# Linear attention over 64 images: context in 64-column tiles, attention in 64x64 tiles, one masking operation a group, and the copy of k moved ahead of the copy of v

## The reference, cut to what matters

```
q, k, v = split(rmsnorm(layernorm(h)) @ w_qkv)           # 4 heads of 32 channels, 64 tokens
k = softmax over tokens of concat(mem_k (4 columns), k)  # 68 columns
v = concat(mem_v, v)
q = softmax over the 32 channels of a head, * 32**-0.5
context = einsum('bhdn,bhen->bhde', k, v)                # 32x32 for each head and image
out = einsum('bhde,bhdn->bhen', context, q)
h = h + rmsnorm(out @ w_out + b_out) + layernorm(h)
```

## Time and profile before

| | us |
|---|---|
| median of 3 runs | 4284.08 (4277.56 to 4299.02) |
| the profiled execution | 4291.21 |
| its span, first to last instruction | 4289.4 |
| attention stage, from first `project` to last `take_out` | 3661.59 to 3784.66 |
| PE busy in the whole span | 3236.5 (75%) |
| mean granted clock of TensorE, as a share of 2.4 GHz | 0.882 |

### The profile page before, as it was taken

How to read it: one execution, slowest core, us unless ns; L and a number is a source line. 1 busy time by engine, 2 the same in 40 slices (tenths; PEclk the granted TensorE clock), 3 DMA queues, 4 the chain that set the end, 5 groups by cost and what they waited for, 6 DMA issues and landing times. The chain is left out here.

```text
span 4289.4 us, 122178 instructions
## 1 busy us (share of the span) xinstructions
PE 3236.5 (75%) x54724; PEld 2080.3 (48%) x54724; DVE 2394.2 (56%) x3232; ACT 2090.2 (49%) x1756; POOL 28.9 (1%) x48
## 2 busy tenths in 40 slices
PE   5968866667888566687876666878869996759777
PEld 4746644456555344575554444755542221743532
DVE  3456669963666589645655996456540001454556
ACT  2123345521666555216765553166659996222322
POOL 0000000000000000000000000000000001000000
PEclk8989988888999889899998898999989998669688
DMA  8979887879999877799998786999985441012053
GB/s 314 349 196 248 226 266 276 300 287 356 364 383 374 307 284 297 272 354 364 391 379 310 290 310 269 357 358 385 387 318 207 179 165 66 1 28 53 1 106 64
DMA packets 181647, 1119.64 MB, mean 261 GB/s; under 512 B 25561, under 2 KB 31905, under 8 KB 107326
## 3 DMA queue, kind: packets, MB, share of 16 engines
q1 hardware_dynamic: 140988, 843.27, 54.3%
q10 hardware_dynamic: 39234, 269.45, 18.1%
q0 software_dynamic: 1024, 1.05, 0.1%
HBM read 708.56 MB, written 405.14 MB: 260 GB/s over the span
## 5 line engine op out<-in xcount | busy, mean ns | idle before, releaser
L604 PEld LDWEIGHTS bank<-fb,arena 64*64 64x64 f32 x16384 | 670.0, 199 | 521.8 <-issue 507.7
L604 PE MATMUL bank<-fb,arena 64*64 64x128 f32 x16384 | 675.4, 294 | 244.8 <-ACT arena L661 196.2
L661 ACT ACTIVATE arena<-bank,pwb 128x1024 f32<-128x1024 f32 x512 | 559.1, 1111 | 475.7 <-PE bank L595 351.3
L705 DVE BATCH_NORM_STATS2 stats<-arena 128x6 f32<-128x512 f32 x1024 | 629.0, 676 | 191.1 <-ACT arena L661 190.8
L595 PE MATMUL bank<-arena,wst 64*64 64x512 f32 x4096 | 625.6, 635 | 12.9 <-issue 12.8
L843 ACT ACTIVATE arena<-arena,shift,scale 128x1024 f32<-128x1024 f32 x384 | 443.7, 1229 | 324.9 <-DMA arena<-y_dram 324.7
L697 DVE STREAM_TRANSPOSE arena<-bank 128x512 f32<-128x512 f32 x512 | 321.1, 684 | 454.2 <-PE bank L581 454.2
L653 ACT ACTIVATE arena<-arena,shift,scale 128x2048 f32<-128x2048 f32 x192 | 401.5, 2093 | 320.0 <-issue 206.1
L805 PE MATMUL bank<-arena,fwq 32*32 32x512 f32 x6144 | 285.2, 746 | 333.6 <-DVE arena L848 333.6
L444 PE MATMUL bank<-arena 64*64 64x128 f32 x8192 | 453.9, 393 | 103.4 <-DVE arena L471 83.6
L444 PEld LDWEIGHTS bank<-arena 64*64 64x64 f32 x8192 | 397.5, 154 | 159.5 <-issue 112.2
(11 more groups left out here) (195 smaller groups left out, 2475.9 us busy)
## 6 DMA issues: line engine op xcount, KB each, us to landing
arena<-y_dram SPq DMA_DIRECT2D x224, 2048.0 KB, 10.3
y_dram<-arena ACTq DMA_DIRECT2D x256, 1024.0 KB, 13.4
arena<-in_w_modes SPq DMA_DIRECT2D x32, 2048.0 KB, 17.5
arena<-spec_in SPq DMA_DIRECT2D x32, 2048.0 KB, 14.6
spec_out<-arena SPq DMA_DIRECT2D x128, 512.0 KB, 14.8
arena<-spec_out SPq DMA_DIRECT2D x116, 512.0 KB, 16.5
spec_in<-arena SPq DMA_DIRECT2D x24, 2048.0 KB, 13.6
spec_in<-arena SPq DMA_DIRECT2D x4, 4096.0 KB, 12.0
```

The costliest lines, as they stand in the source:

```text
L604: mm = pe.matmul(hpx(bank[4 + T % 2 * 2 + i][CHAN[v], :])[:, :, j * S:(j + 1) * S], a2[p % 2][CHAN[i], v, :, 4 * T + j], hpx(fb2[CHAN[i], :]),
L661: act.activation(hpx(yout[u])[:, :, T * BK:(T + 1) * BK], banks[:, 4 + T % 2 * 2:6 + T % 2 * 2, :], ACT.Identity, bias=pwb[:]).then_inc(y_ ...
L705: dve.bn_stats(stats[:, p * 48 + 6 * t:p * 48 + 6 * t + 6], hpx(yout[p % 2])[:, i, T * BK:(T + 1) * BK]).then_inc(y_seen, 1)
```

## The change

Four edits, all in the attention stage.

1. `context` makes for each image two products instead of one, for the heads 0, 1 and the heads 2, 3. Each has 64 columns of k as weights and 64 columns of v moving, and they lie in the two column tiles of the array. All 8 images fit in bank 0. Products of heads of different pairs are no longer computed.
2. `attend` makes for each image two products of 64x64 weights in the tiles (0, 0) and (64, 64), the first into bank 2, the second into bank 3.
3. `mask_context` is one operation of 128x512 numbers, with a mask `pairmask` of 64 columns that DVE makes once ahead of the stage. `copy_att` becomes two operations of 64 partitions each.
4. On ACT `copy_kT(n)` stands behind `copy_att(n-1)` and ahead of `values(n+1)`, instead of at the head of the next turn.

```diff
             def project(g):
                 if g > 1:
                     pe.wait_ge(qT_scaled, g - 1)
-                    pe.wait_ge(ctx_masked, 2 * g - 2)
-                    pe.wait_ge(att_copied, g - 1)
+                    pe.wait_ge(ctx_masked, g - 1)
+                    pe.wait_ge(att_copied, 2 * g - 2)
...
             def context(g):
                 for b in range(GI):
-                    mm = pe.matmul(lane_bank[u][3 * (b // 4)][:, b % 4 * HID:(b % 4 + 1) * HID], kTs[u][:, b, :], vkv[u][b // 4][0:C + MEM, b % 4, :],
-                                   start=True, stop=True)
+                    for a in range(2):
+                        mm = pe.matmul(lane_bank[u][0][ROW[a], b * C:(b + 1) * C], kTs[u][:, b, ROW[a]],
+                                       vkv[u][b // 4][0:C + MEM, b % 4, ROW[a]], start=True, stop=True, tile_position=(0, a * C))
...
             def attend(g):
                 for b in range(GI):
-                    mm = pe.matmul(lane_bank[u][2][:, b * S:(b + 1) * S], ctx_s[u][:, b, :], qT[u][:, b * S:(b + 1) * S], start=True, stop=True)
+                    for a in range(2):
+                        mm = pe.matmul(lane_bank[u][2 + a][ROW[a], b * S:(b + 1) * S], ctx_s[u][ROW[a], b, :],
+                                       qT[u][ROW[a], b * S:(b + 1) * S], start=True, stop=True, tile_position=(a * C, a * C))
...
-                act.activation(attT[u], lane_bank[u][2], ACT.Copy).then_inc(att_copied, 1)
+                for a in range(2):
+                    act.activation(attT[u][ROW[a]], lane_bank[u][2 + a][ROW[a]], ACT.Copy).then_inc(att_copied, 1)
...
             for n in range(TG + 1):
-                if n > 0:
-                    copy_kT(n - 1)
                 if n < TG:
                     exps(n)
                 if n > 0:
                     copy_att(n - 1)
+                if n < TG:
+                    copy_kT(n)
                 if n + 1 < TG:
                     values(n + 1)
...
+            dve.tensor_tensor(pairmask, headmask[:, ROW[0]], headmask[:, ROW[1]], ALU.add).then_inc(mem_max, 1)
...
-                for i in range(2):
-                    dve.tensor_tensor(ctx_s[u][:, 4 * i:4 * i + 4, :], lane_bank[u][3 * i].rearrange("p (b x) -> p b x", b=4),
-                                      row4(headmask, 4, HID), ALU.mult).then_inc(ctx_masked, 1)
+                dve.tensor_tensor(ctx_s[u], lane_bank[u][0].rearrange("p (b x) -> p b x", b=GI),
+                                  row4(pairmask, GI, C), ALU.mult).then_inc(ctx_masked, 1)
```

More of the change, by code:

```diff
@@ L1163, in build @@
         kTs = lanes(GI, HID, parts=C + MEM)
-        ctx_s = lanes(GI, HID)
+        ctx_s = lanes(GI, C)
+        pairmask = at(next_free[0], C)
+        next_free[0] += C
         qs, qT, attT = lanes(4, HID), lanes(BK), lanes(BK)
@@ L1253, in attend @@
                 pe.wait_ge(qT_scaled, g + 1)
-                pe.wait_ge(ctx_masked, 2 * g + 2)
+                pe.wait_ge(ctx_masked, g + 1)
                 for b in range(GI):
-                    mm = pe.matmul(lane_bank[u][2][:, b * S:(b + 1) * S], ctx_s[u][:, b, :], qT[u][:, b * S:(b + 1) * S], start=True, stop=True)
+                    for a in range(2):
+                        mm = pe.matmul(lane_bank[u][2 + a][ROW[a], b * S:(b + 1) * S], ctx_s[u][ROW[a], b, :],
+                                       qT[u][ROW[a], b * S:(b + 1) * S], start=True, stop=True, tile_position=(a * C, a * C))
                 mm.then_inc(att_done, 1)
@@ L1260, in project_out @@
                 u = g % 2
-                pe.wait_ge(att_copied, g + 1)
+                pe.wait_ge(att_copied, 2 * g + 2)
                 for t in range(4):
@@ L1331, in vector_attention @@
                 dve.tensor_tensor(sq[:, h], x_tok[:, h], red[:, 7, h].unsqueeze(2).to_broadcast([P, NT // 2, C]), ALU.mult).then_inc(x_ready, 1)
-            dve.wait_ge(mem_max, 1)
+            dve.wait_ge(mem_max, 2)
             k_of = lambda u: lane_bank[u][1].rearrange("p (b n) -> p b n", b=GI)
```

## The result

| | before | changed |
|---|---|---|
| median of 20 runs, us | 4294.09 (4271.38 to 4306.87) | 4273.86 |
| ratio to before, 95% interval | | 0.9948 (0.9932 to 0.9964) |
| profiled execution, us | 4291.21 | 4278.1 |
| its span, us | 4289.4 | 4276.3 |
| attention stage in it, us | 123.1 | 100.9 |

The change makes the kernel 0.52% faster, 0.36% to 0.68% with the interval. One of the 20 runs of the changed kernel took 10508.57 us and is no part of the ratio; the median of the other 19 is 4271.37 us. In a second series, of 12 runs, the ratio was 0.9957 (0.9935 to 0.9979).

What follows compares the result with a forecast made beforehand. PE was taken as the bound, with handoffs to DVE (mask) and ACT (copy of k). Turns -9.2 us, first context 1.4 us earlier, tail +0.4, `pairmask` +0.2: taken as -10, from 4284.1 to 4274 us, range 4254 to 4290.

Steps and rivals of the forecast that it cites:

- The sum of work at 1.2 GHz: Attention stage: 13.57 us a turn, 9.66 us without project; 91.1 us against 100.26 us from first to last context.
- Context, 2.1 to 2.2 us at 1.2 GHz: Context in 32 records of 64 columns: 2.1 to 2.2 us against 3.65; at 2.4 GHz 1.1 to 1.3 against 2.05.
- Attend 2.0 us: Attend in 32 records of 64x64 weights, 0.0625 us each: 2.0 us against 3.43 us at 1.2 GHz.
- tiles that wait for each other: Rival: tiles of context and attend do not run side by side, 3.8 us each; +18 us, 4302 us; chance 0.05.
- The mask's wait 0.88 us: Between context and attend: one mask operation cuts 1.48 to 0.88 us; at 2.4 GHz DVE is late, mask starts at 2.15 us.
- turn_k waits for the exponentials: After attend: turn_k can start at 5.2 us, attend ends at 5.1 us; 0.1 us of the gain is lost.
- The wait for the copy of k goes: Ahead of context: waits for ACT of 0.94 us and first 1.4 us go; nothing gained in turns at 0.50.
- A change of tile shape: Between products of different tile shapes on PE: costs at most 0.19 us; two new ones a group would be 0.4 us.
- changes paid in full: Changing the tiling mode drains the array: by that rule the two changes a group make the gain 3 us smaller.
- The clock at 0.50 throughout: Attention stage: PE stays at 0.50 of 2.4 GHz from the first context on, turns of 13.4 to 13.9 us; chance 0.5.
- the clock rises in every turn: Rival, attention stage: turns of 10.9 us, -28 us, 4256 us, chance 0.2; in half of the turns 4265 us.
- a stage outside this one: Rest of the kernel: the prediction is wrong if any stage outside the attention stage moves by more than 5 us.

Runs made afterwards that it cites:

- the kernel before with the filling: Kernel before plus 5 products a group, without use for the result, between context and attend; stage 130.2 us.
- the changed kernel with the old order: Changed kernel with the copy of k on ACT back at the head of the next turn; stage 94.9 us.
- early maxima: Changed kernel with a group's two maxima taken one turn earlier on VectorE; median 4261.42 us of 8 runs, ratio to before 0.9919, stage 92.7 us.
- the changed kernel with both edits: Changed kernel with maxima one turn earlier and 3 useless products a group between context and attend; median 4263.98 us of 6 runs, ratio to before 0.9924, stage 81.8 us.
- the kernel before with filling and edit 4: Kernel before plus 5 useless products a group between context and attend, and copy of k ahead of copy of v on ACT; stage 96.6 us.

## Why the prediction was right in sign and small by half

It said 4274 us, 0.23% or 10 us under the median then shown; the changed kernel is 0.52% or 22 us under before. That the 4274 us agree with the measured median of 4273.86 us is luck, by two misses of about the same size: the 3 runs shown then had a median of 4284.1 us where 20 runs have 4294.1 us, and the gain was put 12 us too small. The sum of work at 1.2 GHz was right (a turn of 13.57 us forecast; 13.46 us from the changed kernel's own pieces at that clock, below); the clock was not.

- *Context, 2.1 to 2.2 us at 1.2 GHz; 1.1 to 1.3 us at 2.4 GHz.* Near: 1.98 and 1.15 us. *Attend 2.0 us.* Right: 1.97 us; that gives 0.06 us a record, and no sign of tiles that wait for each other.
- *The mask's wait 0.88 us, and VectorE late at 2.4 GHz.* Right: 0.89 us, and 1.59 us where the mask starts 1.91 us after context (2.15 us forecast).
- *turn_k waits for the exponentials.* Right: 0.15 us at 1.2 GHz, 0.97 us at 2.4 GHz. What it cost in the second case stood in the rival's sum and was right there too.
- *The wait for the copy of k goes.* Right.
- *A change of tile shape at most 0.19 us.* Right: turn_q (L1242) started 0.99 us before the narrow context in the changed kernel (3714.60 and 3715.59) and 0.85 us before the wide one (3722.44 and 3723.29), so at most 0.14 us. The other change, from attend back to turn_k, lies behind the wait for the exponentials and is not measured. Whether the 3 us in all that the prediction names for changes paid in full were lost, these runs can't tell from the scatter of the stage.
- *The clock at 0.50 throughout.* This is the step that failed. It leaned on the self-attention stage, where the clock stays down under full load. In three executions of the changed kernel no full turn was at 0.50. Full load in narrow tiles is no proof that a stage stays at 1.2 GHz, and neither is full load in wide tiles one that it rises: the kernel before with the filling was at 0.50 with PE busy 17.38 of 17.38 us. What the clock did came from the rival "the clock rises in every turn" (a turn of 10.9 us, stage 28 us shorter), which one execution met in full with 10.1 to 10.2 us and two in about half of the turns, for which it had given 4265 us, 19 us under. The prediction gave the clock up in part or nearly all of the turns 0.35. The rival's turn was 0.7 us too long: turn_k started 4.86 us after context instead of 5.1 us, since VectorE was less late, and turn_k and project took 1.67 and 2.12 us instead of 1.85 and 2.36 us, since the clock was up again sooner.

What the experiments showed in its place: the clock of this stage rises and falls within the turns, and what lies between TensorE's products changes how often. In the ten executions without filling it never held through a full turn (PEclk at most 0.85). Once up, it fell in each turn in which PE rested 1.5 to 1.6 us for the mask, and also with shorter pairs of rests: 0.94 and 0.89 us in the changed kernel with the old order, 0.89 and 0.97 us with early maxima. With the copy of k first and the rest at the mask at 0.42 to 0.55 us or filled, it stayed at 1.00 in five, five and four full turns (9.68, 8.99 and, in the kernel before with edit 4, 10.01 us).

The length of the rests alone does not decide it. A rest of 0.97 us in each turn did not lose the clock in the changed kernel with both edits, a single one of 0.94 us lost it in the kernel before with the filling, and in the sixth turn of the kernel before with filling and edit 4 it fell with the rests of the turns in which it had held. What makes it rise is open too, since 17.38 us without a rest did not. Whether the filling holds the clock because the rest is shorter or because of the work that it adds, these runs do not part.

So the gain has two parts. With the clock at 2.4 GHz throughout the narrow tiles and the single mask save 0.33 us a turn, since the turn then waits for VectorE and ScalarE (1.7 us of rest in 9.68 us against 0.6 us in 10.01 us); at 1.2 GHz their context, mask and attend save 16.93 - 13.46 us, 3.5 us (13.46 is the changed kernel's own pieces at 1.2 GHz: 4.98 from context to turn_k, 1.82, 3.91 and 2.75). The profiled pair is 20.8 us apart over seven turns, 3.0 us a turn, with a PEclk of 0.50 to 0.75 before and of 0.60 to 0.84 after. How the 22 us divide among the four edits stays open: edits 1, 2 and 4, each alone, gave a stage of 117 to 119 us, within the scatter of the kernel before (117 to 123 us), and together they gave 88 to 101 us.

The prediction also said that a stage outside this one should not move by 5 us. The span less this stage was 4166 us in the profiled execution before and 4175 us after, but it was 4185 us in the second execution of the kernel before. It scatters by that much without any change, which the sentence had not allowed for. Its mean is 4175.5 us in the two executions before and 4175.3 us in the three after, so no part of the gain shows outside the stage.

## What to carry to other kernels

Where TensorE changes its clock within a loop, the sum of work is only half of a forecast: price each turn at both clocks, read off where the rests of the engine lie, and give the clock's pattern a range, since two executions of one program here differed by 13 us in a stage of 100. Taking away one of two rests of the engine that bounds a loop can bring nothing (118.1 and 130.2 us against 117.1 and 123.1 us of the kernel before) where taking both brought 20 to 27 us (96.6 us), each in one execution. And an engine that is late only at the higher clock (here VectorE, by the maxima) is found by working out the turn at that clock as well.

## What was not expected of the hardware

- One program, unedited, had stages of 100.9, 87.9 and 100.4 us in three executions, by the pattern of TensorE's clock alone. All three began the stage alike: 12.85 us from the first project to the first context in each.
- The clock stayed at 0.50 through 17.38 us in which TensorE was never idle, with 128x128 weights in attend, in the filling and in project_out. In another execution it outlasted a rest of 0.97 us in every turn.
- Useless products went with shorter turns: 4 of them a group in the changed kernel, with 9.68 us a turn against 10.1 to 13.3 us.
